# Two VectorE sums per octet ahead of a halved inverse transform, and another order of patch copies and statistics

## The chip, the core and the metric

The kernel runs on one core of one Trainium2 chip. A time is the device time of one execution in microseconds (us), the median of several. The engines are named TensorE (PE in the profile), VectorE (DVE), ScalarE (ACT), GpSimd (POOL) and SyncE (SP, which issues the transfers).

## What is computed

x is 16 images of 32 channels and 128 x 128 pixels, fp32. The first layer (group norm, a dynamic depthwise convolution, a 1x1 convolution, a residual) isn't touched by the change. The second layer is:

```python
hidden = jnp.einsum('oc,bchw->bohw', w_hidden, x)              # x after group norm; 192 hidden channels
hidden = conv_general_dilated(hidden, w_dw, padding='SAME', feature_group_count=192)   # 3x3, depthwise
q, k, v = jnp.split(hidden, 3, axis=1)                         # 64 channels each
q_fft = jnp.fft.rfft2(to_patch(q))                             # patches of 8 x 8
k_fft = jnp.fft.rfft2(to_patch(k))
out = jnp.fft.irfft2(q_fft * k_fft, s=(8, 8))
out_norm = (out - mean(out, channels)) / sqrt(var(out, channels) + 1e-05)
gated = v * (out_norm * norm_w + norm_b)
x = x + jnp.einsum('oc,bchw->bohw', w_out, gated)
```

The product of two spectra is complex. With a cosine part and a sine part for each frequency it needs four real products: cosine by cosine, sine by cosine, cosine by sine, sine by sine. The real part of the result is a difference of two of them, the other part a sum. Of the 64 coefficients of a patch, 60 belong to 30 pairs of mirrored frequencies, and 4 frequencies are real alone.

## The kernel before

**Two stages.** Stage one (to about 545 us) runs the first layer image by image and writes the normalised result to memory in halves of fp16 (high and low part). Stage two runs 32 units u = 0 to 31, each half an image: 64 rows, thus 8 rows of patches by 16 patches, 128 patches for each of 64 channels of Q, K and V. A unit has two parts. The *front* of unit u (function `front`, one for each engine) makes the hidden values of u and, woven into them, finishes unit u - 1 (the tail): norm over the channels, values, gating, projection, residual. The *spectral* part (function `spectral`) makes the spectra and the inverse transform of u. Every engine's order is written out by hand; engines meet only by semaphores.

**Front.** VectorE's `window(u, r)` copies patch row r (0 to 7) with its border out of the loaded half image `xs` into one of three buffers `win` (line 1102). TensorE's `hidden_group(u, g)` (line 572) multiplies a quarter of a patch row by the hidden weights, 32 groups for a unit, four for each window; ScalarE's `windows_out` (line 810) copies the result out. `window(u, r)` waits until the groups of window r - 2 in this counting, 4 (r - 2) groups, are done, since it fills the buffer that they read. Between groups TensorE runs `v_chunk` (line 587, values, 18 matmuls), `turn` (line 600, transposes the normed result of the tail) and `project` (line 609). For the tail VectorE runs, in eight pieces p: `pixel_stats` (line 1112, four instructions), `variance` (lines 1118 and 1120), `centre` (line 1125), `scale` (line 1132, behind GpSimd's power, line 456), `gate` (line 1137) and `residual` (line 1144). The turn of piece p waits for `scale(p)`.

**Spectral.** For each octet m of 8 channels TensorE makes Q's spectra (`q_octet`, line 647), then K's (`k_octet`, line 659), 32 records each. Channel c of four sits in partitions 32c to 32c + 31: 32 coefficients of the cosine kind in one column block of 128, 32 of the sine kind in the next. ScalarE copies Q's out of PSUM (line 852). VectorE makes two products per octet (line 1197, `quad` 0 and 1), each 512 elements per partition: the four real products of two spectra in four blocks of 128 of the buffer `prod`. `inverse(e)`, e = 0 to 3, turns two octets back: for each of the four blocks (`both`) eight matmuls of 256 columns accumulate into PSUM (line 676), 32 matmuls in all, each of which is two records in the trace. Inverse 0 stands behind octet 2, inverse 1 behind octet 4, inverses 2 and 3 behind octet 7, then the first `v_chunk` of the same unit. ScalarE copies the result to `Y` (line 865). `k_octet(m)` waits for the products of octet m - 2, since there are two PSUM banks for K.

`prod` has room for four octets, and products wait for the inverse that read the place before (`s_inverse_mm`). VectorE's first three window copies of unit u + 1 stand between the two products of octets 4, 5 and 6.

Of the kernel before, what the change touches and what calls it, by code (L numbers as in the profile page):

```python
# [28 lines left out]
TABLES = {"tables": (("identity", 128), ("inverse", 256), ("w_out", 64)),  # L29
# [5 lines left out]
def constants():  # L35

    p = np.arange(128)
# [4 lines left out]
    u, v = np.divmod(np.arange(64), 8)  # L42
# [3 lines left out]
    freq = np.concatenate([pairs, real[:2], pairs, real[2:]])  # L46
    sine = (np.arange(64) >= 32) & (np.arange(64) < 32 + len(pairs))
    angle = 2 * np.pi * ((u[freq][:, None] * u + v[freq][:, None] * v) % 8) / 8
    wave = np.where(sine[:, None], np.sin(angle), np.cos(angle)).reshape(64, 8, 8)
    spectra = np.zeros((9, 64, 10, 10), np.float64)  # L50
    for tap in range(9):
# [9 lines left out]
    cosines, sines = np.cos(angle), np.sin(angle)  # L61
    paired = np.arange(32)[:, None] < len(pairs)
    inverse = np.concatenate([np.where(paired, 2, 1) * cosines[:32], np.where(paired, 2 * sines[:32], 0), np.where(paired, 2 * sines[:32], 0),
                              np.where(paired, -2, 1) * cosines[32:]], axis=1) / 64
    out["inverse"] = np.tile(inverse, (4, 1)).astype(np.float32)
# [3 lines left out]
def build(nc, t, out):  # L69
# [13 lines left out]
    LAST = 2 * NB - 1  # L83
# [8 lines left out]
    with ctx:  # L92
# [4 lines left out]
        def semaphore(name):  # L97
            return ctx.enter_context(nc.semaphore(name))
# [86 lines left out]
        s_prod_ready = semaphore("prod_ready")  # L185
        s_inverse_mm = semaphore("inverse_mm")
# [277 lines left out]
        def _(pe):  # L464
# [173 lines left out]
            def spectral(u, tail):  # L638
# [25 lines left out]
                def inverse(e):  # L664
                    pe.wait_ge(s_prod_ready, 16 * u + 4 * e + 4)
                    if 0 < e < 3:
                        pe.wait_ge(s_y_ready, 16 * u + 4 * e)
                    if e == 0 and tail is not None:
                        pe.wait_ge(s_gated, 8 * u)
                        pe.wait_ge(s_t_copied, 8 * u)  # L670
                    if e == 3 and tail is not None:
                        pe.wait_ge(s_res_done, 4 * u)
                    for both in range(4):
                        for c in range(4):
                            for lam in range(2):
                                mm = pe.matmul(i_banks(e)[c][64 * lam:64 * lam + 64, 256 * (e % 2):256 * (e % 2) + 256],  # L676
                                               small["inverse"][32 * c:32 * c + 32, 64 * both:64 * both + 64],
                                               at(prod[32 * c:32 * c + 32, :], 2048 * (e % 2) + 128 * both + 64 * lam, [512, 4], [1, 64]),
                                               start=both == 0, stop=both == 3)
                    mm.then_inc(s_inverse_mm, 1)  # L680
# [202 lines left out]
        def _(dve):  # L883
# [262 lines left out]
            def front(u, tail):  # L1146
# [17 lines left out]
                for p in range(3):  # L1164
                    pixel_stats(tail, p)
                    variance(tail, p)
                    if p == 1:
                        centre(tail, 0)
                windows()
                scale(tail, 0)  # L1170
                centre(tail, 1)
                scale(tail, 1)
# [14 lines left out]

            def spectral(u, tail):
                for n in range(16):
                    m, quad = n // 2, n % 2  # L1190
                    if quad == 0:
                        dve.wait_ge(s_q_copied, 8 * u + m + 1)
                        dve.wait_ge(s_k_mm, 8 * u + m + 1)
                        if positive(4 * u + m // 2 - 1):
# [4 lines left out]
                                      at(q_sb[m % 2], 256 * quad, [0, 2], [128, 2], [1, 128]), ALU.mult).then_inc(s_prod_ready, 1)  # L1199
                    if n == 1 and tail is not None:  # L1200
                        gate(tail, 3, 1)
                    if n == 3 and tail is not None:
                        residual(tail, 3)
                    if u < LAST and n in (8, 10, 12):
                        window(u + 1, n // 2 - 4)
# [53 lines left out]
```

## Time and profile before

| | us |
|---|---|
| median of 3 runs | 2357.64 (2355.62 to 2362.33) |
| the profiled execution | 2366.28 |
| its span, first to last instruction | 2364.4 |
| TensorE busy (matmul records) | 2236.0 |
| VectorE busy | 1613.8 |
| ScalarE busy | 1454.2 |
| inverse transform, line 676, 8192 records | 255.6 |
| products, line 1197, 512 instructions | 337.2 |
| mean granted TensorE clock | 0.972 |

The span is one execution from its first to its last instruction; the profiled execution's own time is 1.9 us longer, and it lies 8.6 us above the median of the runs without a profile. Busy times of matmuls are modelled and overlap with pipelining, so start-to-start distances are safer for prices. The granted clock is 1.00 at TensorE's full 2.4 GHz and 0.50 at 1.2 GHz.

### The profile page before, as it was taken

What the parts mean: (1) busy time and instruction counts of PE and PEld (TensorE: products, weight loads), DVE (VectorE), ACT (ScalarE), POOL (GpSimd) and SP (SyncE); (2) the same over time, 40 slices, a digit from 0 to 9 for tenths busy, and PEclk for the clock granted to TensorE, in tenths of its full rate; (3) what the DMA queues carried; (4) which work ended last, traced back from release to release, by engine and by line L of the source; (5) the groups of instructions that cost most, each with busy time, mean ns of one, the idle gap of its engine ahead of it and who ended that gap; (6) DMA issues with size and microseconds to landing.
All of it is one profiled execution on the core that took longest, in us unless ns stands there. A gap on an engine that the chain in (4) does not pass through costs nothing.

```text
span 2364.4 us, 107028 instructions
## 1 busy us (share of the span) xinstructions
PE 2236.0 (95%) x48375; PEld 1443.6 (61%) x48375; DVE 1613.8 (68%) x4058; ACT 1454.2 (62%) x2629; POOL 486.3 (21%) x323
## 2 busy tenths in 40 slices
PE   7888888868999999999999999999999999999997
PEld 3333333346666666777676766667666666667664
DVE  5566766646777767767677667777777777777775
ACT  3456655566666666666666666666666666666662
POOL 1000000002222222222222222222222222222222
PEclk9889988978999999999999999999999999999999
DMA  7689888784333333333333333333333333333312
GB/s 140 168 212 234 226 204 219 214 200 103 75 76 76 76 76 76 79 81 76 84 73 79 76 84 80 84 81 84 76 84 76 83 78 76 76 76 76 76 43 50
DMA packets 60409, 248.63 MB, mean 105 GB/s; under 512 B 12393, under 2 KB 12658, under 8 KB 53810
## 3 DMA queue, kind: packets, MB, share of 16 engines
q1 hardware_dynamic: 59954, 241.78, 43.3%
q8 instruction: 381, 6.24, 1.1%
q14 instruction: 74, 0.61, 0.1%
HBM read 140.02 MB, written 101.72 MB: 102 GB/s over the span
## 4 chain that ended last, share of the span: by engine, by line
PE 84%; DVE 7%; ACT 4%; issue 4%; DMA 1%; SPq 0%; POOL 0%; POOLq 0%; ACTq 0%
PE bank L587 18%; PE bank L527 16%; PE bank L676 11%; PE bank L659 10%; PE bank L647 9%; PE bank L572 7%; PE bank L600 7%; PE bank L609 5%; DVE arena L1112 3%; ACT arena L865 2%; DVE arena L1132 1%; DVE arena L1125 1%; ACT arena L819 1%; DVE arena L1102 1%; ACT arena L724 1%
## 5 line engine op out<-in xcount | busy, mean ns | idle before, releaser
L456 POOL TENSOR_TENSOR arena<-arena 128x8 f32<-128x8 f32 x256 | 462.1, 1805 | 1357.6 <-DVE arena L1118 1352.6
L587 PE MATMUL bank<-arena 128*64 128x512 f16 x4608 | 689.9, 393 | 0.0
L810 ACT ACTIVATE arena<-bank 100x512 f32<-100x512 f32 x1024 | 606.6, 628 | 95.4 <-PE bank L572 75.1
L1197 DVE TENSOR_TENSOR arena<-bank,arena 128x512 f32<-128x512 f32 x512 | 337.2, 687 | 207.8 <-issue 174.0
L572 PEld LDWEIGHTS bank<-arena 128*36 128x36 f16 (+1 forms) x8192 | 330.5, 104 | 232.4 <-issue 23.5
L527 PE MATMUL bank<-arena 32*32 32x508 f32 (+1 forms) x9216 | 382.9, 649 | 55.4 <-issue 40.6
L572 PE MATMUL bank<-arena 128*36 128x128 f16 (+1 forms) x8192 | 390.5, 221 | 17.4 <-DVE arena L1102 11.5
L819 ACT ACTIVATE arena<-bank,arena 128x256 f32<-128x256 f32 x512 | 261.1, 560 | 119.9 <-PE bank L600 119.4
L852 ACT ACTIVATE arena<-bank 128x512 f32<-128x512 f32 x256 | 153.2, 598 | 265.7 <-PE bank L647 265.2
L1112 DVE BATCH_NORM_STATS2 arena<-arena 128x6 f32<-128x128 f32 x1024 | 221.7, 279 | 121.3 <-ACT arena L865 121.3
L647 PE MATMUL bank<-arena 100*32 100x128 f32 x8192 | 277.5, 274 | 5.2 <-issue 3.9
L659 PE MATMUL bank<-arena 100*32 100x128 f32 x8192 | 278.3, 274 | 0.7 <-issue 0.7
L1137 DVE TENSOR_TENSOR arena<-arena,bank 128x512 f32<-128x512 f32 x256 | 175.3, 685 | 145.9 <-ACT arena L819 145.8
L865 ACT ACTIVATE arena<-bank 128x256 f32<-128x256 f32 x512 | 155.3, 391 | 185.6 <-PE bank L676 185.6
L587 PEld LDWEIGHTS bank<-arena 128*64 128x64 f16 x4608 | 206.3, 109 | 96.0 <-ACT arena L865 10.5
L527 PEld LDWEIGHTS bank<-arena 32*32 32x32 f32 x9216 | 142.4, 107 | 194.9 <-issue 163.6
L659 PEld LDWEIGHTS bank<-arena 100*32 100x32 f32 x8192 | 222.0, 109 | 55.5 <-issue 26.4
L676 PE MATMUL bank<-arena 32*64 32x256 f32 x8192 | 255.6, 380 | 0.2
L647 PEld LDWEIGHTS bank<-arena 100*32 100x32 f32 x8192 | 220.4, 109 | 21.2 <-issue 5.0
L676 PEld LDWEIGHTS bank<-arena 32*64 32x64 f32 x8192 | 180.8, 129 | 50.3 <-issue 16.8
L600 PEld LDWEIGHTS bank<-arena 128*128 128x128 f32 x1024 | 133.7, 195 | 119.3 <-DVE arena L1132 88.7
L600 PE MATMUL bank<-arena 128*128 128x128 f32 x1024 | 181.4, 300 | 18.1 <-DVE arena L1132 10.9
(112 smaller groups left out, 1605.1 us busy)
## 6 DMA issues: line engine op xcount, KB each, us to landing
arena<-xn_d SPq DMA_DIRECT2D x128, 536.2 KB, 4.8
xn_d<-arena SPq DMA_DIRECT2D x130, 260.0 KB, 4.5
x_d<-arena SPq DMA_DIRECT2D x64, 512.0 KB, 8.3
arena<-x_d SPq DMA_DIRECT2D x128, 256.0 KB, 4.2
out<-arena SPq DMA_DIRECT2D x128, 256.0 KB, 2.7
arena<-x_in SPq DMA_DIRECT2D x32, 544.0 KB, 9.6
arena<-x_in SPq DMA_DIRECT2D x32, 528.0 KB, 9.4
arena<-spectra_in SPq DMA_DIRECT2D x1, 384.0 KB
```

The costliest lines, as they stand in the source:

```text
L456: pool.tensor_tensor(tiny["rstd"][:, slot], tiny["var_eps"][:, slot], powers, ALU.pow).then_inc(s_root, 1)
L527: mm = pe.matmul(at(psum_of(t, r)[32 * c:32 * c + 32, :], low, [W, 4], [1, high - low]), conv_w[b % 2][32 * r:32 * r + 32, 32 * tap:32 * t ...
L572: mm = pe.matmul(ring[g % len(ring)][low:high, 128 * i:128 * i + 128], w[:, first + low:first + high], hidden_w, start=True, stop=True)
L587: mm = pe.matmul(v_banks[chunk % 3][64 * s:64 * s + 64, :], v_w[:, 64 * tap:64 * tap + 64], at(xs[u % 3], row * WP + 32 * k + dx, [32 * WP ...
L600: tr = pe.transpose(t_bank[:, 128 * i:128 * i + 128], at(Y, 8 * k + 4 * jr + i, [32, 128]), ident)
L647: mm = pe.matmul(q_bank[32 * c:32 * c + 32, first:first + 128], G_q[0:WIN, 64 * ch + 32 * part:64 * ch + 32 * part + 32], hwin[0:WIN, 128 ...
L659: mm = pe.matmul(k_banks[m % 2][32 * c:32 * c + 32, first:first + 128], G_k[0:WIN, 64 * ch + 32 * part:64 * ch + 32 * part + 32], hwin[0:W ...
L676: mm = pe.matmul(i_banks(e)[c][64 * lam:64 * lam + 64, 256 * (e % 2):256 * (e % 2) + 256], small["inverse"][32 * c:32 * c + 32, 64 * both: ...
L810: act.activation(h_rows[0:WIN, :, first:first + 4], ring[g % len(ring)][0:WIN, :].rearrange("p (i c) -> p c i", i=4), ACT.Copy).then_inc(s ...
L819: ins = act.activation(at(gated[jr], 256 * lam, [32, 8], [8, 4], [1, 8]), at(banks[4], 64 * lam, [8, 8], [128, 4], [1, 8]), ACT.Identity, ...
L1112: ins = dve.bn_stats(T["pixel_stats"][:, first:first + 6], at(Y, 2048 * s + 4 * p + j, [32, 64], [1, 2]))
L1197: dve.tensor_tensor(prod[:, first:first + 512].rearrange("p (a b x) -> p a b x", a=2, b=2), at(k_banks[m % 2], 256 * quad, [128, 2], [0, 2 ...
```

## The change

VectorE gets a new function `spectrum(u, m)` behind the two products of each octet. It waits for its own products (`s_prod_ready`), then issues two instructions of 256 elements per partition (two blocks of 128, one for each of two groups of channels): a `scalar_tensor_tensor` that multiplies the fourth block by a sign per partition (-1 for the 30 pairs, 1 for the two real frequencies in the block) and adds the first, and a `tensor_tensor` that adds the second and third. Both write in place, and the second signals the new semaphore `s_spectrum`. `inverse(e)` waits for that instead of `s_prod_ready` and runs over two blocks instead of four: 16 matmuls instead of 32. The real frequencies' table rows are recast as half sums and half differences so that the same two sums serve them; the table `inverse` has 128 columns instead of 256, and one column `cross_sign` is new.

On VectorE two orders change as well. The first three window copies of the next unit stand behind all products of the unit instead of between those of octets 4 to 6. And in the front's beginning, where three sets of statistics came first, the fourth window copy (r = 3) now stands behind the first set, and the second and third set stand behind the first centring and the second one. TensorE's, ScalarE's, GpSimd's and SyncE's order of steps is the same.

```diff
+        s_spectrum = semaphore("spectrum")
...
                 def inverse(e):
-                    pe.wait_ge(s_prod_ready, 16 * u + 4 * e + 4)
+                    pe.wait_ge(s_spectrum, 8 * u + 2 * e + 2)
...
-                    for both in range(4):
+                    for part in range(2):
                         for c in range(4):
                             for lam in range(2):
...
-                                               start=both == 0, stop=both == 3)
+                                               start=part == 0, stop=part == 1)
...
-                for p in range(3):
-                    pixel_stats(tail, p)
-                    variance(tail, p)
-                    if p == 1:
-                        centre(tail, 0)
+                pixel_stats(tail, 0)
+                variance(tail, 0)
                 windows()
+                centre(tail, 0)
+                pixel_stats(tail, 1)
+                variance(tail, 1)
                 scale(tail, 0)
                 centre(tail, 1)
+                pixel_stats(tail, 2)
+                variance(tail, 2)
                 scale(tail, 1)
                 windows()
...
+            def spectrum(u, m):
+
+                first = 1024 * (m % 4)
+                dve.wait_ge(s_prod_ready, 16 * u + 2 * m + 2)
+                dve.scalar_tensor_tensor(at(prod, first, [512, 2], [1, 128]), at(prod, first + 384, [512, 2], [1, 128]),
+                                         small["cross_sign"], at(prod, first, [512, 2], [1, 128]), ALU.mult, ALU.add)
+                dve.tensor_tensor(at(prod, first + 128, [512, 2], [1, 128]), at(prod, first + 128, [512, 2], [1, 128]),
+                                  at(prod, first + 256, [512, 2], [1, 128]), ALU.add).then_inc(s_spectrum, 1)
...
+                    if quad == 1:
+                        spectrum(u, m)
                     if n == 1 and tail is not None:
                         gate(tail, 3, 1)
                     if n == 3 and tail is not None:
                         residual(tail, 3)
-                    if u < LAST and n in (8, 10, 12):
-                        window(u + 1, n // 2 - 4)
+                if u < LAST:
+                    for r in range(3):
+                        window(u + 1, r)
```

VectorE, octets 5 and 6 of a unit's spectral part, before: the products (line 1197) with a window copy (line 1102) between each two.

```order
L1197 TENSOR_TENSOR arena<-bank,arena 128x512 [waits inverse_mm,k_mm,q_copied]
L1102 COPY arena<-arena 128x1600 [waits hidden_mm]
L1197 TENSOR_TENSOR arena<-bank,arena 128x512
L1197 TENSOR_TENSOR arena<-bank,arena 128x512 [waits inverse_mm,k_mm,q_copied]
L1102 COPY arena<-arena 128x1600 [waits hidden_mm]
L1197 TENSOR_TENSOR arena<-bank,arena 128x512
```

VectorE, the last octet and what follows it, now; line numbers of the changed kernel (1207 the products, 1193 and 1195 the sums, 1101 the window copy, 1111 the statistics).

```order
L1207 TENSOR_TENSOR arena<-bank,arena 128x512 [waits inverse_mm,k_mm,q_copied]
L1207 TENSOR_TENSOR arena<-bank,arena 128x512
L1193 SCALAR_TENSOR_TENSOR arena<-arena 128x2x128 [waits prod_ready]
L1195 TENSOR_TENSOR arena<-arena 128x2x128
L1101 COPY arena<-arena 128x1600 [waits xs_in1,hidden_mm]
L1101 COPY arena<-arena 128x1600 [waits hidden_mm] x2
L1111 BN_STATS arena<-arena 128x6 [waits y_ready]
```

The sums follow each pair of products behind a wait for them, and the three copies follow the last sums.

VectorE, the beginning of the front, before, from the end of the first set of statistics to the first scaling (line 1132).

```order
L1118 TENSOR_SCALAR arena<-arena 128x8 [waits pixel_stats]
L1120 COPY arena<-arena 128x8
L1112 BN_STATS arena<-arena 128x6 x4
L1118 TENSOR_SCALAR arena<-arena 128x8 [waits pixel_stats]
L1120 COPY arena<-arena 128x8
L1125 TENSOR_TENSOR arena<-arena 128x128x4 [waits pixel_mean]
L1112 BN_STATS arena<-arena 128x6 x4
L1118 TENSOR_SCALAR arena<-arena 128x8 [waits pixel_stats]
L1120 COPY arena<-arena 128x8
L1102 COPY arena<-arena 128x1600 [waits hidden_mm]
L1132 TENSOR_TENSOR arena<-arena 128x128x4 [waits y_centred,root]
```

The same place now (each of these lines has a number one lower).

```order
L1117 TENSOR_SCALAR arena<-arena 128x8 [waits pixel_stats]
L1119 COPY arena<-arena 128x8
L1101 COPY arena<-arena 128x1600 [waits hidden_mm]
L1124 TENSOR_TENSOR arena<-arena 128x128x4 [waits pixel_mean]
L1111 BN_STATS arena<-arena 128x6 x4
L1117 TENSOR_SCALAR arena<-arena 128x8 [waits pixel_stats]
L1119 COPY arena<-arena 128x8
L1131 TENSOR_TENSOR arena<-arena 128x128x4 [waits y_centred,root]
```

The copy, with its wait for hidden groups, moved ahead of the second statistics, and one set of statistics moved behind the first scaling.

TensorE, the end of the spectral part, before: K of the last octet, the inverses 2 and 3, the values.

```order
L659 MATMUL bank<-arena 32x128 [waits prod_ready]
L659 MATMUL bank<-arena 32x128 x15
L676 MATMUL bank<-arena 64x256 [waits y_ready,prod_ready]
L676 MATMUL bank<-arena 64x256 x31
L676 MATMUL bank<-arena 64x256 [waits res_done,prod_ready]
L676 MATMUL bank<-arena 64x256 x31
L587 MATMUL bank<-arena 64x512 [waits y_ready]
```

And now:

```order
L658 MATMUL bank<-arena 32x128 [waits prod_ready]
L658 MATMUL bank<-arena 32x128 x15
L675 MATMUL bank<-arena 64x256 [waits y_ready,spectrum]
L675 MATMUL bank<-arena 64x256 x15
L675 MATMUL bank<-arena 64x256 [waits res_done,spectrum]
L675 MATMUL bank<-arena 64x256 x15
L586 MATMUL bank<-arena 64x512 [waits y_ready]
```

The steps stand as before; each inverse has half its matmuls and waits for the sums.

## Rows read from the trace of the kernel before

**Rows 1.** The page's costliest groups: the inverse (busy us, mean ns, idle before).

```profile
L676 PE MATMUL bank<-arena 32*64 32x256 f32 x8192 | 255.6, 380 | 0.2
```

**Rows 2.** Spectral, front: length; busy PE, PEld, DVE, ACT, POOL; clock; DMA.

```profile
1448.00:1472.60 24.60, 24.41 (x778) 19.78 (x777) 14.26 (x23) 10.46 (x24) 0.00 (x0) 1.00 0.23 50
1472.60:1504.40 31.80, 31.47 (x448) 19.30 (x440) 26.06 (x77) 26.02 (x48) 14.48 (x8) 1.00 0.43 102
```

**Rows 3.** TensorE in order of time: start, us, line, shape, records, idle before.

```profile
1456.59 2.00 PE L676 MATMUL bank<-arena 32*64 32x256 f32 x64
1458.52 1.08 PE L659 MATMUL bank<-arena 100*32 100x128 f32 x32
1459.42 1.06 PE L647 MATMUL bank<-arena 100*32 100x128 f32 x32
...
1467.95 1.06 PE L659 MATMUL bank<-arena 100*32 100x128 f32 x32
1468.94 3.74 PE L676 MATMUL bank<-arena 32*64 32x256 f32 x128
1472.61 2.26 PE L587 MATMUL bank<-arena 128*64 128x512 f16 x18
```

**Rows 4.** VectorE in order of time, products and gate of the same spectral part.

```profile
1451.22 1.29 DVE L1197 TENSOR_TENSOR arena<-bank,arena 128x512 f32<-128x512 f32 x2 [0.64 <-issue]
1452.43 0.68 DVE L1137 TENSOR_TENSOR arena<-arena,bank 128x512 f32<-128x512 f32 x1
```

**Rows 5.** VectorE: a step behind its own predecessor; an operand from memory.

```profile
1445.54 0.69 DVE L1125 TENSOR_TENSOR arena<-arena 128x512 f32<-128x512 f32 x1
1446.33 0.70 DVE L1132 TENSOR_TENSOR arena<-arena 128x512 f32<-128x512 f32 x1
...
34.73 0.21 DVE L1022 TENSOR_SCALAR arena<-arena 128x1 f32<-128x1 f32 x1
34.86 0.68 DVE L947 BATCH_NORM_STATS2 arena<-arena 128x6 f32<-128x512 f32 x1
```

**Rows 6.** VectorE, then TensorE, at the beginning of the front.

```profile
1474.04 0.87 DVE L1112 BATCH_NORM_STATS2 arena<-arena 128x6 f32<-128x128 f32 x4 [3.62 <-ACT arena L865]
1474.95 0.17 DVE L1118 TENSOR_SCALAR arena<-arena 128x8 f32<-128x8 f32 x1
...
1477.82 0.57 DVE L1102 COPY arena<-arena 128x1600 f16<-128x1600 f16 x1
1478.31 0.69 DVE L1132 TENSOR_TENSOR arena<-arena 128x512 f32<-128x512 f32 x1
...
1481.86 0.68 DVE L1137 TENSOR_TENSOR arena<-arena,bank 128x512 f32<-128x512 f32 x1
...
1475.83 0.40 PE L572 MATMUL bank<-arena 128*64 128x128 f16 x8
1479.05 0.71 PE L600 MATMUL bank<-arena 128*128 128x128 f32 x4 [0.33 <-DVE arena L1132]
...
1483.64 0.65 PE L587 MATMUL bank<-arena 128*64 128x512 f16 x4
```

**Rows 7.** TensorE behind idle gaps, and busy us and granted clock thereafter.

```profile
73.08 1.07 PE L527 MATMUL bank<-arena 32*32 32x508 f32 x7 [1.58 <-issue]
...
73.60:77.00 3.40, 3.40 (x48) 0.94 (x35) 0.53 (x4) 0.00 (x0) 0.89 (x2) 0.50 1.00 225
...
80.40:83.80 3.40, 3.40 (x65) 0.81 (x33) 0.45 (x1) 3.40 (x6) 0.00 (x0) 0.55 0.18 40
...
560.77 0.43 PE L647 MATMUL bank<-arena 100*32 100x128 f32 x8 [2.90 <-issue]
...
561.70:565.10 3.40, 3.40 (x74) 2.34 (x74) 1.29 (x2) 0.36 (x1) 0.00 (x0) 0.56 0.02 5
565.10:568.50 3.40, 3.40 (x106) 2.16 (x92) 0.00 (x0) 2.03 (x8) 0.00 (x0) 1.00 0.02 5
...
2325.39 0.71 PE L600 MATMUL bank<-arena 128*128 128x128 f32 x4 [1.56 <-DVE arena L1132]
```

More of the change, by code:

```diff
@@ L26 @@
 TINY = 1e-30
-TABLES = {"tables": (("identity", 128), ("inverse", 256), ("w_out", 64)),
+TABLES = {"tables": (("identity", 128), ("inverse", 128), ("w_out", 64), ("cross_sign", 1)),
           "weights": (("quarter_mean", 128), ("eye", 32), ("w1", 128), ("w2", 4), ("dyn_w", 36), ("conv1", 32),
@@ L45, in constants @@
     pairs = np.flatnonzero(mirror > np.arange(64))
[L46 to L49, printed above, removed]
+    angle = 2 * np.pi * ((u[:, None] * u + v[:, None] * v) % 8) / 8
+    cosine, sine = np.cos(angle), np.sin(angle)
+    half_sum, half_diff = (cosine[real[:2]] + cosine[real[2:]]) / 2, (cosine[real[:2]] - cosine[real[2:]]) / 2
+    wave = np.concatenate([cosine[pairs], half_sum, sine[pairs], half_diff]).reshape(64, 8, 8)
     spectra = np.zeros((9, 64, 10, 10), np.float64)
@@ L60, in constants @@
     out["row_mask"] = np.pad(np.repeat(row[:, None] == np.arange(8), 64, axis=1), ((0, 24), (0, 0))).astype(np.float32)
[L61 to L65, printed above, removed]
+    inverse = np.concatenate([2 * cosine[pairs], 2 * half_sum, 2 * sine[pairs], 2 * half_diff]).reshape(2, 32, 64)
+    out["inverse"] = np.tile(np.concatenate([inverse[0], inverse[1]], axis=1) / 64, (4, 1)).astype(np.float32)
+    out["cross_sign"] = np.tile(np.where(np.arange(32) < len(pairs), -1, 1)[:, None], (4, 1)).astype(np.float32)
     return out
@@ L676, in inverse @@
                                 mm = pe.matmul(i_banks(e)[c][64 * lam:64 * lam + 64, 256 * (e % 2):256 * (e % 2) + 256],
-                                               small["inverse"][32 * c:32 * c + 32, 64 * both:64 * both + 64],
-                                               at(prod[32 * c:32 * c + 32, :], 2048 * (e % 2) + 128 * both + 64 * lam, [512, 4], [1, 64]),
-                                               start=both == 0, stop=both == 3)
+                                               small["inverse"][32 * c:32 * c + 32, 64 * part:64 * part + 64],
+                                               at(prod[32 * c:32 * c + 32, :], 2048 * (e % 2) + 128 * part + 64 * lam, [512, 4], [1, 64]),
+                                               start=part == 0, stop=part == 1)
                     mm.then_inc(s_inverse_mm, 1)
```

## The prediction, made before the changed kernel ran

> **What bounds the kernel now.** I read the page first: the inverse matmuls of line 676 are 8192 records with 255.6 us of modelled time [rows 1]. A share of the whole span says little, so next I read the busy times of one unit in the second stage. There are 32 units (16 images, two halves), some 56.4 us each. The spectral part lasts 24.6 us and the front part 31.8 us; TensorE is busy 24.41 and 31.47 of these, VectorE 14.26 and 26.06, and the granted clock is 1.00 in both [rows 2]. So TensorE sets the pace throughout, and VectorE has 10 us free in exactly the part where the change gives it work. The third view, TensorE in order of time at the end of that spectral part, gives the prices. One inverse step holds TensorE from 1456.59 to 1458.52, 1.93 us; two in a row from 1468.94 to 1472.61, 3.67 us; one group of 32 records for Q or K takes 0.90 us from start to start [rows 3].
>
> **What is removed.** Each inverse step has half the matmuls. From the two prices, a step is 3.67 / 2 = 1.83 us and a change of kind costs 0.1 us more. Half is 0.92 us, so one unit loses 4 x 0.92 = 3.67 us of TensorE, and 32 units lose 117 us. That would be the gain if TensorE never had to wait.
>
> **What is added on VectorE.** Per octet (8 channels, two products) there are now two more instructions of 256 elements per partition, the first behind a wait for VectorE's own products. A product starts every 0.60 us (two of them 1.29, one 0.69) [rows 4]. A 512-element operation lasts 0.69 us and an 8-element one 0.17 [rows 5, 6], so 256 elements last 0.43; the next starts 0.09 us before the end, as with the products, thus 0.34 us after the start. An instruction that waits for VectorE's own predecessor starts 0.10 us behind its end (1445.54 + 0.69, then 1446.33), not 0.09 before it, so the wait costs 0.19 [rows 5]. The per-partition sign is an operand from memory: an operation with one, at 34.73, lets its successor in after 0.13 us; without one I would take 0.07, since its duration is 0.21 [rows 5]. The fused multiply-add of that size isn't in the trace. Its bounds are 0.34 (no price for the operand) and 0.69 (as dear as 512 elements); I take 0.40, since line 1022 is the nearest row. An octet is then 0.60 + 0.79 + 0.40 + 0.34 = 2.13 us on VectorE, where it was 1.2. TensorE needs 1.8 us for the Q and K of an octet, so VectorE now falls behind between the inverses.
>
> **The spectral part, followed in order.** Times count from the start of Q at 1448.13 in the unit of [rows 2]. The first product starts at 3.09, as before [rows 4]. Octet 0 ends its issue at 5.22; the gate product (line 1137) now stands behind its sums and runs at 5.22 instead of 4.30 [rows 4]. The projection waits for it only with its second half, and TensorE loses nothing. Octet 1 runs at 5.81, the residual at 7.94, octets 2, 3 and 4 at 8.54, 10.67 and 12.80. The sums for inverse 0 are there at 8.02 (TensorE wants them at 8.46), those for inverse 1 at 12.88 (wanted at 13.16). On TensorE, each shorter inverse moves all that follows forward by 0.92: K of octet 5, 6 and 7 end at 15.25, 17.10 and 19.06. VectorE takes octet 5 at 15.37, 6 at 17.50 and 7 at 19.63, by then 0.45 us behind. Inverse 2 runs from 18.97 to 19.9. Inverse 3 needs the sums of octet 7: 19.63 + 0.60 + 0.79 + 0.40 + 0.42 = 21.84, and with 0.1 us of hand-over it starts at 21.93. **TensorE stands idle for 2.0 us** between the last two inverses, where it had no gap [rows 3]. Inverse 3 ends at 22.87, where both ended at 24.48: the spectral part gains 1.61 us, not 3.67. With the bounds of the multiply-add, 0.34 gives 1.8 and 0.69 gives some -0.3 (0.29 us more in each of eight octets, of which the 0.44 us that VectorE waits before octet 5 absorbs a part).
>
> **The window copies** leave the products (three of 0.57 us, some 0.5 each in the queue) and stand behind them, from 21.76 to 23.3. VectorE would otherwise wait there until about 24.3 for inverse 3 and ScalarE's copies. Cost nothing; TensorE wants the first window some 2 us later, behind the values' matmuls. If that cover were gone they would cost 1.5 us a unit.
>
> **The front part's new order** puts a window copy behind the first statistics. Before, three sets of statistics came first: they began at 1474.04, the copy at 1477.82, the first scaling at 1478.31, and TensorE's turn of it at 1479.05, after a wait of 0.33 [rows 6]. The copy reuses the buffer of the oldest window, thus waits for the fourth hidden group (index 3), which ends at 1475.83 + 0.40 = 1476.23 [rows 6]. The statistics before it are over at about 1475.10. So VectorE now waits 1.2 us in a place where it never waited: window 1476.35, centring 1476.84, second statistics 1477.44, scaling 1478.50, 0.19 later than before although one set of statistics less stands in front. I charge 0.2 us a unit, 31 times. Further on VectorE runs 1.0 us late. The step with the least room is the first gate: it ends at 1481.86 + 0.68 = 1482.54, and the values that need it start at 1483.64 [rows 6]. Its 1.1 us just cover the delay, so nothing more is charged; if they didn't, it would be up to 1 us a unit. SP's queue has the same order of transfers, with waits on the same steps. The last front part, without windows, gains 1.2 us once, since its wait of 1.56 us for the first scaling [rows 7] mostly goes.
>
> Sum so far: 32 x 1.61 - 31 x 0.2 + 1.2 = 46.5 us.
>
> **What the new gap does to the clock.** This term halves the gain. In the first stage and the end TensorE has idle gaps of every length, and I compared each with the granted clock behind it. After the gap of 1.58 us at 73.08 the next stretch has 0.50; after the 2.90 us at 560.77, matmuls of the spectral part itself run at 0.56 on average from 561.70 on, for 3.4 us, then at 1.00; after 1.56 us at 2325.39 the clock stays full [rows 7]. Of eight gaps between 1.4 and 1.9 us that began at the full clock, from 73.08 to 2325.39, five were followed by the lower level (1.2 GHz) and three were not. All nine between 2.5 and 6 us were, and none of about 1.2 us. The new gap of 2.0 us lies between these sets. I take 6 in 10, 19 to 20 of 32 units. A stretch like that of 561.70 costs half of 3.4 us, 1.7; part of it falls into the rest of the gap, so 1.6. That is 32 us: the work it slows (inverse 3, values, hidden groups) is bound by TensorE, and nothing hides it. The net gain is 46.5 - 32 = 14.5 us. Against the profiled execution's own 2366.28 us that is 2352; the median of the runs shown is 8.6 us lower, and the second stage, where all this lies, repeats unit by unit, so I subtract from the median: **2343 us**, -0.6%.
>
> The Trainium skill (TensorE: Matmul & The Clock Gate, "Why this matters for your kernels") asks only that TensorE's idle gaps between bursts of matmuls stay under some 3 us, and by that rule a gap of 2.0 us would leave the clock alone. The rows contradict it here, with gaps of 1.58 and 2.90 us before 0.50. By the rule the time would be the first rival's.
>
> **Rivals.** (1) The gap costs no clock. For it: three of the eight short gaps; the units' matmuls use more of the array's rows than the first stage's. Against it: five of eight, and a unit of the same code at 560.77. It gives 2357.6 - 46.5 = 2311; with the cheaper multiply-add 2305. (2) Slower: the low clock outlives one stretch. After 73.60 it holds for three stretches of 3.4 us with TensorE busy in all [rows 7]. If the values and hidden groups don't bring it back at once, a second stretch costs 1.7 us more, thus 19 x 3.3 = 63 us: 2357.6 - 46.5 + 63 = 2374. It decides from 1.45 us lost per unit on average. Against it: after 561.70 one stretch was enough. (3) VectorE is dearer than priced. With the multiply-add at 0.69 the spectral part is 0.3 us slower than before, and its longer gap draws the clock down too: 2357.6 + 32 x 0.3 + 5 + 32, about 2404. Only the far bound supports it. (4) The change does nothing because another engine holds the unit: with TensorE at 24.41 of 24.6 us that is hardly possible, 2358.
>
> **How the numbers follow.** Chances: forecast 0.46, rival (1) 0.28, (2) 0.18, (3) 0.04, (4) 0.04. The range reaches from 2305 (rival 1 at its cheap bound) to 2370, most of the way to rival (2), and leaves out the rest of it and rival (3). The forecast's own range is 2325 to 2358 (from 4 to 9 units in 10 hit, hand-overs 0.1 us off). A measurement of this kernel tells 0.3%, 7 us, from no change. Faster: 0.28, 0.38 of the forecast's 0.46 and 0.02 of the rest, 0.68. Same: 0.07 of the forecast, 0.03 of rival (2) and 0.03 of (4), 0.13. Slower: 0.19.
>
> **What would show it.** In the changed profile: 4096 records for the inverse; an idle time of about 2.0 us before the fourth inverse, released by VectorE's second sum; sums that last 0.43 and 0.49 us; a wait of VectorE for the hidden groups before the fourth window; granted clock under 1.00 in most 57 us slices of the second stage, and a mean near 0.96 instead of 0.97. It is wrong if the gap is under 1.4 us, or if units with the gap keep 1.00 throughout.

## The result: slower, 2391.6 us

| | before | changed |
|---|---|---|
| median, us | 2359.59 (2355.62 to 2362.33, 4 runs) | 2391.57 (2384.37 to 2398.07, 4 runs) |
| ratio | | 1.0126 (1.0102 to 1.015) |
| span of the profiled execution | 2364.4 | 2388.1 |
| mean granted clock | 0.972 | 0.960 |

The forecast was 2343 (2305 to 2370). What was forecast for the inverse, the idle gap and the clock is in the trace; some 48 us more are there too. (Of the ten executions of e10 below one ran slow, at a granted clock of 0.557 in 3389 us; the ratios leave it out.) The changed kernel's page, costliest groups; line numbers are one lower than before up to line 1160. First the inverse (as in [rows 1]), then ScalarE's copy of the hidden groups, then the statistics:

```profile
L675 PE MATMUL bank<-arena 32*64 32x256 f32 x4096 | 157.5, 414 | 56.4 <-DVE arena L1195 55.1
L809 ACT ACTIVATE arena<-bank 100x512 f32<-100x512 f32 x1024 | 691.8, 751 | 80.6 <-PE bank L571 77.7
L1111 DVE BATCH_NORM_STATS2 arena<-arena 128x6 f32<-128x128 f32 x1024 | 265.5, 323 | 47.5 <-ACT arena L864 47.5
```

The same two groups on the page of the kernel before:

```profile
L810 ACT ACTIVATE arena<-bank 100x512 f32<-100x512 f32 x1024 | 606.6, 628 | 95.4 <-PE bank L572 75.1
L1112 DVE BATCH_NORM_STATS2 arena<-arena 128x6 f32<-128x128 f32 x1024 | 221.7, 279 | 121.3 <-ACT arena L865 121.3
```

The inverse has half its records, and 55.1 us of idle time before it that VectorE's second sum ends. That was expected. But instructions that the change doesn't touch have become dearer: ScalarE's copy by 123 ns, one statistics instruction by 44 ns. Nothing in the forecast prices that.

**The spectral part** (the end on TensorE; the second gate and the projection that stands early in it; the end on VectorE; one unit at full clock; it answers to [rows 3, 4]):

```profile
1068.72 1.06 PE L658 MATMUL bank<-arena 100*32 100x128 f32 x32
1069.71 1.13 PE L675 MATMUL bank<-arena 32*64 32x256 f32 x32
1072.67 1.13 PE L675 MATMUL bank<-arena 32*64 32x256 f32 x32 [1.83 <-DVE arena L1195]
1073.73 2.27 PE L586 MATMUL bank<-arena 128*64 128x512 f16 x18
...
1055.72 0.68 DVE L1136 TENSOR_TENSOR arena<-arena,bank 128x512 f32<-128x512 f32 x1
1056.14 1.39 PE L608 MATMUL bank<-arena 128*64 128x512 f32 x4
...
1070.48 1.28 DVE L1207 TENSOR_TENSOR arena<-bank,arena 128x512 f32<-128x512 f32 x2
1071.79 0.48 DVE L1193 SCALAR_TENSOR_TENSOR arena<-arena 128x256 f32<-128x256 f32 x1
1072.20 0.42 DVE L1195 TENSOR_TENSOR arena<-arena 128x256 f32<-128x256 f32 x1
1072.53 1.54 DVE L1101 COPY arena<-arena 128x1600 f16<-128x1600 f16 x3
```

The last octet's products end at 1071.76, the sums follow at 1071.79 and 1072.20, and the last inverse starts 0.05 us behind them after 1.83 us of idle time. From the start of Q to the values (1050.56 to 1073.73) it is 23.17 us, where the kernel before took 24.48 in the unit of the rows and 24.2 to 24.9 in its neighbours. The window copies run in VectorE's free time.

The projection of the tail (line 608) takes longer too. Before, in the same place, 5.57 us behind the start of Q:

```profile
1453.70 1.08 PE L609 MATMUL bank<-arena 128*64 128x512 f32 x4
```

The gate product now stands behind the sums of octet 0 and ends at 1056.40, so the projection's second half starts at 1056.45, 0.32 us behind the first, where before the two started within 0.01 us. The K octet behind the projection starts 6.90 us after Q instead of 6.58. So 0.32 us of the 1.6 forecast are lost here, in every unit.

**The front part** of the next unit, VectorE, then TensorE (it answers to [rows 6]):

```profile
1075.16 1.05 DVE L1111 BATCH_NORM_STATS2 arena<-arena 128x6 f32<-128x128 f32 x4 [1.08 <-ACT arena L864]
...
1077.51 0.58 DVE L1101 COPY arena<-arena 128x1600 f16<-128x1600 f16 x1 [1.02 <-PE bank L571]
...
1084.69 0.68 DVE L1136 TENSOR_TENSOR arena<-arena,bank 128x512 f32<-128x512 f32 x1
...
1080.63 0.71 PE L599 MATMUL bank<-arena 128*128 128x128 f32 x4 [0.68 <-DVE arena L1131]
...
1085.42 0.65 PE L586 MATMUL bank<-arena 128*64 128x512 f16 x4
...
1088.62 1.67 PE L608 MATMUL bank<-arena 128*64 128x512 f32 x4
```

The window copy waits for its hidden group, as forecast. Four statistics last 1.05 us instead of 0.87. TensorE waits 0.68 us at the first turn (0.33 before); the first gate ends at 1085.37, 0.05 before the values that need it, which had 1.1 us of room; the first projection spans 1.67 us, 1.03 in the kernel before, because it waits for the second gate. The front lasts 33.25 us instead of 31.95. So **a unit at full clock takes 56.42 us, what it took before (56.38)**: 1.3 us won in the spectral part, 1.3 lost in the front.

**The clock.** Two stretches of the changed kernel around its gap, [rows 7] for comparison: one unit with the low clock, one without.

```profile
1469.70:1473.10 3.40, 1.57 (x48) 0.97 (x56) 3.36 (x8) 1.22 (x4) 0.00 (x0) 0.95 0.36 83
1473.10:1476.50 3.40, 3.40 (x39) 1.40 (x26) 1.64 (x6) 1.22 (x4) 0.00 (x0) 0.55 0.34 80
1476.50:1479.90 3.40, 3.40 (x64) 2.00 (x60) 1.45 (x6) 2.20 (x4) 1.64 (x1) 1.00 1.10 254
...
1069.70:1073.10 3.40, 1.57 (x52) 0.98 (x56) 3.33 (x9) 1.22 (x4) 0.00 (x0) 1.00 0.26 57
1073.10:1076.50 3.40, 3.40 (x74) 1.94 (x57) 2.27 (x9) 1.46 (x5) 0.00 (x0) 1.00 0.68 160
```

The gap is the same in both. Behind the one the granted clock is at its lower level (1.2 GHz) for 3.4 us and the unit takes 58.02 us, behind the other it stays at 2.4. All of units 1 to 31 have the gap, and 20 of them have such a stretch; 20 x 1.6 = 32 us, all of the loss. (Unit 0 has no tail and another pattern of gaps; stretches are counted in units 1 to 31 from here on.)

### The profile page after: what moved, and what is told of

Read it like the earlier page. It is cut to its first block, busy times and chain, and to the rows that moved or that the text cites. A ratio compares the mean times of both kernels' runs of the same rounds, so it can differ in the third digit from the quotient of the medians.

```text
span 2388.1 us, 99348 instructions
## 1 busy us (share of the span) xinstructions
PE 2191.1 (92%) x44279; PEld 1360.5 (57%) x44279; DVE 1868.8 (78%) x4570; ACT 1531.1 (64%) x2629; POOL 495.1 (21%) x323
## 4 chain that ended last, share of the span: by engine, by line
PE 73%; DVE 18%; issue 5%; ACT 3%; DMA 1%; POOL 0%; SPq 0%; ACTq 0%; DVEq 0%; POOLq 0%
PE bank L586 19%; PE bank L526 16%; PE bank L658 7%; PE bank L571 7%; PE bank L608 6%; PE bank L646 6%; PE bank L599 5%; DVE arena L1207 5%; PE bank L675 5%; DVE arena L1111 4%; DVE arena L1131 2%; DVE arena L1124 2%; DVE arena L1195 2%; DVE arena L1101 1%; DVE arena L1136 1%
## 5 line engine op out<-in xcount | busy, mean ns | idle before, releaser
L455 POOL TENSOR_TENSOR arena<-arena 128x8 f32<-128x8 f32 x256 | 470.9, 1839 | 1374.2 <-DVE arena L1117 1373.8
L809 ACT ACTIVATE arena<-bank 100x512 f32<-100x512 f32 x1024 | 691.8, 751 | 80.6 <-PE bank L571 77.7
L586 PE MATMUL bank<-arena 128*64 128x512 f16 x4608 | 708.9, 403 | 4.8 <-DVE arena L1136 1.0
L1207 DVE TENSOR_TENSOR arena<-bank,arena 128x512 f32<-128x512 f32 x512 | 328.7, 684 | 54.0 <-issue 53.0
L1111 DVE BATCH_NORM_STATS2 arena<-arena 128x6 f32<-128x128 f32 x1024 | 265.5, 323 | 47.5 <-ACT arena L864 47.5
L586 PEld LDWEIGHTS bank<-arena 128*64 128x64 f16 x4608 | 212.5, 112 | 121.2 <-issue 40.7
L675 PE MATMUL bank<-arena 32*64 32x256 f32 x4096 | 157.5, 414 | 56.4 <-DVE arena L1195 55.1
L1131 DVE TENSOR_TENSOR arena<-arena 128x512 f32<-128x512 f32 x256 | 189.8, 742 | 21.0 <-POOL arena L455 1.2
```

What stands on the lines that cost most here:

```text
L455: pool.tensor_tensor(tiny["rstd"][:, slot], tiny["var_eps"][:, slot], powers, ALU.pow).then_inc(s_root, 1)
L586: mm = pe.matmul(v_banks[chunk % 3][64 * s:64 * s + 64, :], v_w[:, 64 * tap:64 * tap + 64], at(xs[u % 3], row * WP + 32 * k + dx, [32 * WP ...
L809: act.activation(h_rows[0:WIN, :, first:first + 4], ring[g % len(ring)][0:WIN, :].rearrange("p (i c) -> p c i", i=4), ACT.Copy).then_inc(s ...
L1111: ins = dve.bn_stats(T["pixel_stats"][:, first:first + 6], at(Y, 2048 * s + 4 * p + j, [32, 64], [1, 2]))
L1207: dve.tensor_tensor(prod[:, first:first + 512].rearrange("p (a b x) -> p a b x", a=2, b=2), at(k_banks[m % 2], 256 * quad, [128, 2], [0, 2 ...
```

## The experiments

The theories: **address** (the small tables shrank by 127 columns, so all buffers behind them in the arena moved by 127 fp32 words, an odd number, and accesses there cost more), against **contention** (VectorE's new work slows ScalarE and the front); **clock** (the gap itself brings the low level), against another cause; and what each of the two changed orders costs. The column `pad` is never read. Each kernel was timed beside the kernel before on the same chip; the ratios compare across the groups. Low stretches are counted in one profiled execution of each kernel. In these executions unit 1 starts its Q at anything from 584 to 600 us, e1 at 584 and the changed kernel at 594, so some 10 us between two single traces can come from stage one; unit lengths are the surer measure.

### e1 to e4: addresses and clock

e1, on the changed kernel:

```diff
-TABLES = {"tables": (("identity", 128), ("inverse", 128), ("w_out", 64), ("cross_sign", 1)),
+TABLES = {"tables": (("identity", 128), ("inverse", 128), ("w_out", 64), ("cross_sign", 1), ("pad", 127)),
```

> The changed kernel with 127 unused columns behind its small tables, so that everything behind them in the arena lies at the address it had in the kernel before (the change alone moved it by 127 fp32 words, an odd number). Address theory: ScalarE's copy of the hidden groups goes from 751 ns back to 628, the statistics from 323 to 279, a unit at full clock from 56.4 us to about 55.1, and the time from 2391.6 to about 2353; some 20 units still meet the low clock. Rival (VectorE's new load slows ScalarE and the front by contention): durations and time stay, about 2391.

Measured: 2336.19 us, ratio 0.9909 (0.9892 to 0.9927). The page has the old durations again:

```profile
L810 ACT ACTIVATE arena<-bank 100x512 f32<-100x512 f32 x1024 | 608.3, 632 | 103.0 <-PE bank L572 84.7
L1112 DVE BATCH_NORM_STATS2 arena<-arena 128x6 f32<-128x128 f32 x1024 | 221.8, 278 | 40.1 <-ACT arena L865 40.1
```

The same work at other addresses is 55 us faster than the changed kernel by the medians, 51 by the ratios. Front 32.29, spectral 23.15, unit 55.44 us. Contention falls. That this came out below the 2353 expected is in the main the clock: 10 low stretches, not some 20. From the Q of unit 1 to the Q of unit 31 the two traces differ by 45.9 us: 30 x 0.98 for the units and 1.6 for each of the ten stretches fewer. The other 5 to 9 us of the medians' difference aren't traced to a cause.

e2, on the kernel before:

```diff
-TABLES = {"tables": (("identity", 128), ("inverse", 256), ("w_out", 64)),
+TABLES = {"tables": (("identity", 128), ("inverse", 256), ("w_out", 64), ("pad", 1)),
```

> The kernel before with one unused column behind its small tables: everything behind them moves by 4 bytes, nothing else changes. Address theory: ScalarE's copy goes from 628 to about 751 ns, the statistics from 279 to 323, and the time from 2358 to some 2370 to 2395. Rival (contention from the new sums): nothing changes, 2358.

Measured: 2376.39 us, ratio 1.0092 (1.0066 to 1.0119), with no low stretch in these units.

```profile
L811 ACT ACTIVATE arena<-bank 100x512 f32<-100x512 f32 x1024 | 685.5, 751 | 62.1 <-PE bank L573 59.9
L1113 DVE BATCH_NORM_STATS2 arena<-arena 128x6 f32<-128x128 f32 x1024 | 265.0, 323 | 119.5 <-ACT arena L866 119.5
```

One unused column costs the old kernel 20 us, and the two durations are to the nanosecond those of the changed kernel. The front is 32.53 instead of 31.95.

e3 is e1 with `("pad", 1)`.

> The changed kernel with one unused column: the front's buffers then start at a multiple of 16 bytes, where the kernel before has them 8 bytes past one and the changed kernel 12 bytes past one. If groups of 8 bytes matter, durations are as in e1 (628 and 279 ns), time about 2353. If lines of 16 bytes matter, ScalarE's copy, which writes four fp32 side by side, is faster still than 628 ns, and the time is a few us below e1.

Measured: 2341.54 us, ratio 0.994 (0.9919 to 0.9961). Neither expectation quite: the copy is faster as 16-byte lines would have it, the time is not.

```profile
L810 ACT ACTIVATE arena<-bank 100x512 f32<-100x512 f32 x1024 | 582.2, 600 | 124.3 <-PE bank L572 93.4
L1112 DVE BATCH_NORM_STATS2 arena<-arena 128x6 f32<-128x128 f32 x1024 | 221.4, 278 | 39.6 <-ACT arena L865 39.6
```

Counted from the arena's start, the front's buffers begin 0, 8 or 12 bytes past a multiple of 16 in e3, e1 and the changed kernel (the latter also in e2). ScalarE's copy writes groups of four fp32: 600, 632, 751 ns. The statistics read pairs of fp32: 278, 278, 323 ns. The 323 is a mean of two kinds. Shortest, median and longest duration of all 1024 statistics, changed kernel and kernel before:

```profile
L1111 DVE BATCH_NORM_STATS2 arena<-arena x1024: 262/330/404, 562.3 to 2364.4; 128x6 f32<-128x128 f32 x171
L1112 DVE BATCH_NORM_STATS2 arena<-arena x1024: 267/277/296, 568.9 to 2340.6; 128x6 f32<-128x128 f32 x171
```

Of the four instructions of a piece the first and third read pairs that begin 12 bytes past a multiple of 16 and reach over the next one; they last 368 ns on average. The second and fourth read pairs that begin at 4; they last 277. Before, at 8 and 0, they last 281 and 277. So in one and the same kernel only the reads that cross a multiple of 16 bytes are dear.

A unit takes 55.41 us, as in e1, with 12 low stretches against 10.

e4, on e1:

```diff
-                    for part in range(2):
+                    for part in (0, 1, 0, 1) if e == 2 else (0, 1):
```

> As e1, and the third inverse of each unit (the one ahead of the idle gap) is done twice over, same values: 0.92 us more of matmuls in a gap of 1.8 us. It does more work than e1 and none earlier. Clock theory (the gap draws the clock down in about 20 units, 1.6 us each): no low stretches in the second stage, 32 us faster than e1, about 2321. Rival (low stretches have another cause, or cost nothing): as e1 or slower, 2353.

Measured: 2327.9 us, ratio 0.9869 (0.9849 to 0.9889): 8 us faster than e1, beside it on the same chip, with 32 x 0.92 us more of matmuls. The gap, and the second stage's busy times and clock:

```profile
1498.43 2.00 PE L676 MATMUL bank<-arena 32*64 32x256 f32 x64
1501.39 1.13 PE L676 MATMUL bank<-arena 32*64 32x256 f32 x32 [0.96 <-DVE arena L1196]
...
600.00:1200.00 600.00, 582.76 (x12104) 399.91 (x12094) 502.91 (x1264) 397.95 (x784) 161.56 (x88) 1.00 0.35 82
1200.00:1800.00 600.00, 582.54 (x12188) 401.17 (x12186) 501.79 (x1257) 394.29 (x779) 158.03 (x86) 1.00 0.35 81
```

No low stretch in these units, every unit some 55.44 us. The clock theory holds: with the gap cut to 0.96 us the stretches are gone, with 1.83 some units have one. The size was expected for 20 stretches; e1 has 10. From the Q of unit 1 to that of unit 31 e4 is 13.5 us shorter than e1; the medians differ by 8, and e4's stage one was 7.6 us longer in the profiled execution.

### e5 to e7: the two orders

e5 is e1 with the first hunk of the change in `front` undone: three statistics, then the window copy.

> As e1_shifted_back, with the front's beginning in the order of the kernel before (three sets of statistics, then the fourth window copy). My theory: the new order costs a wait of VectorE for the fourth hidden group, 32.29 us a front where the order before has 31.94; so the front returns to about 31.95 and the time is 11 us below e1 (2336), about 2325, give or take 10 for how many units meet the low clock. Rival (the front's 0.35 us come from VectorE's load, not from this order): front and time stay at 32.3 and 2336.

Measured: 2322.0 us, ratio 0.9843 (0.9827 to 0.9859). Front 31.95, unit 55.10; 7 low stretches. The new order costs 0.34 us a unit. At the shifted addresses it costs more: e2 has the old order and a front of 32.53, the changed kernel the new one and 33.25, a difference of 0.72.

e6 is e1 with the window copies back between the products:

```diff
-                if u < LAST:
-                    for r in range(3):
-                        window(u + 1, r)
+                    if u < LAST and n in (8, 10, 12):
+                        window(u + 1, n // 2 - 4)
```

> As e1_shifted_back, with the three window copies back between the products of octets 4 to 6. My theory: VectorE is the bound at the end of the spectral part, so 3 x 0.49 us stand in the chain ahead of the last inverse: spectral part 23.15 + 1.0 to 1.5 us, idle gap 2.8 to 3.3 us, the low clock in nearly all units, 30 x 1.2 + 20 x 1.6, thus 2385 to 2410. Rival (VectorE has enough room there): 2336.

Measured: 2403.26 us, ratio 1.0182 (1.0145 to 1.0219).

```profile
1478.75 1.13 PE L676 MATMUL bank<-arena 32*64 32x256 f32 x32
1482.46 1.85 PE L676 MATMUL bank<-arena 32*64 32x256 f32 x32 [2.58 <-DVE arena L1196]
...
600.00:1200.00 600.00, 562.52 (x11342) 380.29 (x11332) 477.94 (x1194) 375.08 (x746) 149.22 (x81) 0.97 0.34 78
1200.00:1800.00 600.00, 565.56 (x11152) 380.23 (x11150) 482.18 (x1221) 382.54 (x751) 158.44 (x87) 0.97 0.34 77
```

The gap is 2.58 us in the unit shown, 2.80 in most and 2.36 to 3.14 in all from unit 1 to 30. Each of these 30 units has a low stretch and takes 58.0 us. (The last unit has no window to copy; its gap is 1.83 and its clock stays full.) Moving the copies behind the products is worth 67 us beside e1 by the medians, 64 by the ratios.

e7 is e1 with this beginning of the front:

```diff
                 pixel_stats(tail, 0)
                 variance(tail, 0)
-                windows()
                 centre(tail, 0)
                 pixel_stats(tail, 1)
                 variance(tail, 1)
+                windows()
                 scale(tail, 0)
```

> As e1_shifted_back, with the fourth window copy behind the second set of statistics, where its hidden group is done. My theory: the first scaling comes some 0.6 us earlier than in either order and TensorE's wait at the first turn goes, front 32.29 to about 31.65, time 20 us below e1, about 2316 give or take 10 for the low clock. Rival: another wait takes its place and the front stays above 31.9.

Measured: 2311.11 us, ratio 0.9794 (0.9774 to 0.9815). Front 31.61, 3 low stretches. VectorE's first scaling and TensorE's first turn:

```profile
1446.60 0.69 DVE L1132 TENSOR_TENSOR arena<-arena 128x512 f32<-128x512 f32 x1
...
1447.78 0.71 PE L600 MATMUL bank<-arena 128*128 128x128 f32 x4
```

The scaling ends at 1447.29, half a microsecond before TensorE gets to the turn, and the wait is gone.

### e8 and e12: the last inverse without sums

e8 is e7 with, besides a table of four blocks `[cos, sin, sin, sign * cos]`:

```diff
-                    pe.wait_ge(s_spectrum, 8 * u + 2 * e + 2)
+                    if e < 3:
+                        pe.wait_ge(s_spectrum, 6 * u + 2 * e + 2)
+                    else:
+                        pe.wait_ge(s_prod_ready, 16 * u + 16)
...
-                    for part in range(2):
+                    for part in range(2 if e < 3 else 4):
...
-                    if quad == 1:
+                    if quad == 1 and m < 6:
```

> e7 and, for the last inverse of each unit, no sums: it runs over four blocks as in the kernel before, with a table that matches. TensorE does 0.92 us more, VectorE four sums fewer at the end. My theory: the gap ahead of the last inverse falls from 1.8 us to 0.5 to 0.9, no unit meets the low clock, the spectral part is 22.6 us (23.15 in e1), and the time is 2285 to 2300. Rival (the gap is not the reason of the low clock, or the extra matmuls eat the gain): e7's time or above.

Measured: 2286.22 us, ratio 0.9694 (0.9674 to 0.9714), the lowest median of all.

```profile
1202.54 1.12 PE L680 MATMUL bank<-arena 32*64 32x256 f32 x32
1204.07 2.00 PE L680 MATMUL bank<-arena 32*64 32x256 f32 x64 [0.41 <-DVE arena L1212]
1206.00 0.88 PE L588 MATMUL bank<-arena 128*64 128x512 f16 x6
```

The gap is 0.41 us, the spectral part 22.60, no low stretch. Halving three inverses of four beats halving all.

e12 is e8 with one unused column instead of three.

> e8_last_four with the front's buffers at a multiple of 16 bytes (one unused column instead of three). ScalarE's copy falls from 632 to 598 ns. The front is bound by TensorE there, so no change of the time: 2286 give or take 5. If ScalarE holds back some hidden groups, 2 to 10 us less.

Measured: 2289.3 us, ratio 0.9681 (0.9636 to 0.9727). The copy takes 600 ns (633 in e8), and the time is the same, as the first case has it.

### e9 to e11: which buffer, and whether the terms add

e9 is e1 with one word taken ahead of `hwin` and one ahead of `Y`:

```diff
+        take(1)
         hwin = take(128 * 128)
...
+        take(1)
         Y = take(64 * 64)
```

> As e1_shifted_back, but hwin, q_sb and prod (hidden values, Q's copy, products) start 4 bytes further on; Y and all behind it stay. Address theory, by buffer: ScalarE's copy into hwin is back at 751 ns, statistics (278) and scalings (692) stay fast. If ScalarE's copy is what lengthens the front of the changed kernel (33.27 us against 32.29), the front is above 33 us and the time 25 to 35 us above e1 (2336). If VectorE's chain of statistics does it, front and time stay at 32.3 and 2336 and e10 shows them.

(With both words Y begins at a multiple of 16 bytes, as in e3, not where e1 has it; by e3 its durations are the same there.) Measured: 2346.16 us, ratio 0.9935 (0.9911 to 0.9959). Front 32.41 at full clock, so 0.12 above e1, and 13 low stretches. The time is 10 us above e1 by the medians, 6 by the ratios: neither the 25 to 35 of the one case nor the nothing of the other, but much nearer to the second.

```profile
L812 ACT ACTIVATE arena<-bank 100x512 f32<-100x512 f32 x1024 | 683.5, 751 | 75.5 <-PE bank L574 73.5
L1114 DVE BATCH_NORM_STATS2 arena<-arena 128x6 f32<-128x128 f32 x1024 | 222.0, 278 | 43.5 <-ACT arena L867 43.5
```

e10 is e1 with one word ahead of `Y` and one behind it, so that Y alone begins 12 bytes past a multiple of 16.

> As e1_shifted_back, but Y, gated, res and the late half image start 4 bytes further on; hwin and the buffers beside it stay. By buffer: ScalarE's copy stays at 632 ns, statistics go to some 323 and scalings to 740. If VectorE's chain to the first turn is what lengthens the front, it is up by 0.6 us or more and the time 20 us or more above e1; if ScalarE's copy is, the front stays at 32.3 us and the time at 2336, give or take 10.

(The text on record says that gated, res and the late half image move as well. The second word moves them by another 4 bytes.) Measured: 2362.46 us, ratio 1.0005 (0.998 to 1.003). Front 33.13.

```profile
L812 ACT ACTIVATE arena<-bank 100x512 f32<-100x512 f32 x1024 | 611.8, 634 | 105.9 <-PE bank L574 87.2
L1114 DVE BATCH_NORM_STATS2 arena<-arena 128x6 f32<-128x128 f32 x1024 | 265.0, 321 | 40.1 <-ACT arena L867 40.1
```

The first turn now waits 0.68 us (0.45 in e1) and the first projection spans 1.66 (1.24), as in the changed kernel. ScalarE's copy has the larger difference per instruction and, with Q's copy and the products moved beside it, 0.12 us of effect; VectorE's statistics, centring and scaling on Y have 0.84 of the 0.97 us. Ahead of its copies ScalarE still waits for TensorE (73.5 us in all in e9), whereas TensorE waits for what VectorE makes of Y.

e11 is the changed kernel with e4's edit.

> The changed kernel at its own addresses, with the third inverse of each unit done twice as in e4. If the address term and the clock term simply add, no unit meets the low clock, a unit takes 56.42 us, and the time is about 2391.6 - 19 x 1.6 = 2361. If the longer front has to do with the low clock, the time is below that.

Measured: 2359.54 us, ratio 0.9974 (0.9951 to 0.9997). Fronts 33.27, units 56.44 us, no low stretch. The length of a unit and the price of a stretch add as expected. The number of stretches doesn't carry over: the same filler takes away 20 here (32 us by the medians) and 10 in e1 (8 us).

## Why the prediction was wrong

| full clock, us | front | spectral | unit | low stretches |
|---|---|---|---|---|
| before | 31.95 | 24.45 | 56.38 | 0 |
| changed | 33.25 | 23.17 | 56.42 | 20 |
| e1, its addresses restored | 32.29 | 23.15 | 55.44 | 10 |
| e5, e1 with the old front | 31.95 | 23.15 | 55.10 | 7 |
| e7, the copy one set later | 31.61 | 23.15 | 54.76 | 3 |
| e8, last inverse on four blocks | 31.61 | 22.60 | 54.21 | 0 |

(Fronts run from the first values' matmul to Q's first, spectral parts from there to the next values; medians of the units without a low stretch; stretches of units 1 to 31.)

- **The step that failed is a term that the sum of 46.5 us puts at nothing.** The sum has terms for instructions added, removed and reordered, and takes all other instructions at their durations before, without a reason. The smaller tables move the buffers behind them by an odd number of words, and VectorE's steps on `Y` and ScalarE's copies got dearer. With the new order in the front that costs 0.97 us a unit, 30 us in all.
- **The front's cover was used up.** The forecast charged 0.2 us for the new order and held that the first gate's 1.1 us "just cover the delay". With e1 it is 0.34 a unit: 0.13 at the first turn (0.45 us of waiting for 0.32 in e5) and 0.21 at the first projection, which spans 1.24 us instead of 1.03. With slower statistics ahead of the gate the cover was gone, as the text had priced ("it would be up to 1 us a unit"). The two don't simply add: the order alone costs 0.34 (e1 against e5), the addresses alone 0.58 (e2 against the kernel before), both together 1.30, so 0.38 of it belongs to neither alone.
- **The spectral part** was forecast to gain 1.61 us and gained 1.3. The forecast said of the projection that waits for the second gate that "TensorE loses nothing"; it loses 0.32 us, in the changed kernel as in all the variants that keep the sums there. The halved inverse, too, was mis-sized: 1.06 us from start to start for 0.92, since the change of kind of 0.1 is paid on each. Both together bring the K of octet 5 0.4 us later than forecast. VectorE then wins some back (an octet takes 2.06 us for 2.13), and the last inverse starts at 22.11 for 21.93. The rest of the order was right: gap 1.83 us for 2.0, sums 0.49 and 0.42 us as forecast.
- **That e1 lies near the forecast is in part luck.** With the addresses restored the kernel takes 2336 us, within 0.3% of 2343. But its units gain some 14 us less than forecast (spectral part 10, front 4), and it has 10 low stretches where 19 to 20 were priced, 16 us less lost; the two errors cancel.
- **The clock term** was right in kind and in price: 1.6 us a stretch (58.02 against 56.42). That 20 units were hit for the 19 to 20 forecast is chance, since the same gap hits 10 in e1 and 3 in e7. In the changed kernel eleven stretches in a row stand 58.0 us apart; in e1, whose units are 55.44 us long, they come singly or in pairs. So the gap alone doesn't set the share. The unit's length may have to do with it (units of 56.42 us: 20 hits; 56.29 in e10: 11; 55.44: 10; 55.10: 7; 54.76: 3), but no run isolates it and each number is of one execution; what sets the share stays open, and a share read off eight gaps of the first stage couldn't tell it. (The forecast's "none of about 1.2 us" passes over the gap of 1.20 at 2348.13 in the trace before, behind which, after a further 0.55 us of idle time, the clock was at 0.50 from 2349.9.) The Trainium skill (TensorE: Matmul & The Clock Gate, "Why this matters for your kernels") permits gaps up to some 3 us; these runs contradict it: 1.83 us was enough in some units, 0.96 in none.
- **The rivals.** Rival (1), no clock loss, is out by e4 and e11. Rival (2), a second low stretch, didn't occur: all in the second stage lasted 3.4 us. The time ended beyond it for a reason that none of them had.

In sum: 32 x 1.3 us gained in the spectral part, some 11 lost by the front's order, 30 by the addresses (18 of them alone, 12 only with the new order), 32 by the clock. That makes 31 us slower; 32 were measured.

## What to carry to other kernels

List what an edit moves in memory as well as in the queues: a table that grows or shrinks ahead of others shifts them all, and one word can cost as much as an edit brings (20 us in e2, against the 21 that e1 gains on the kernel before). Where work moves from the bound engine to another, follow the last item of each loop, since there nothing is left to hide the new steps; leaving the old form for that one item can be the best split. A step that "waits only with its second half" has a price too, if its halves ran side by side before. And an idle gap of about two microseconds on TensorE can be priced twice, by itself and by the clock behind it; filling it even with useless matmuls paid here (8 us in e4, 32 in e11).

## What the runs showed of the hardware

- Access cost by start address, in bytes past a multiple of 16 from the arena's start: ScalarE writing groups of four fp32, 512 per partition out of PSUM, 600 ns at 0, 632 at 8, 751 at 12. VectorE's statistics on pairs of fp32, 278 ns at 0 and 8, 323 at 12; its scalings of groups of four in place, 690 at 0, 692 at 8, 742 at 12. The Trainium skill (SBUF — State Buffer, the note on cachelines in "Door 1: The DMA port swizzle") tells of lines of 16 bytes and a penalty for each access that goes on to another line. It also wants at least two accesses in a line for full bandwidth. Both fit: at 12 bytes each group of four is split into one and three, and ScalarE's copy and the scaling are slow; at 8 it is split into two and two, which costs ScalarE 32 ns and VectorE's scaling nothing clear; and of the statistics only those whose pairs are split are slow, 368 ns for 277.
- How much longer an instruction gets doesn't set the price here: 119 ns more on 32 ScalarE copies a unit cost 0.12 us (e9), some 40 to 50 ns more on each of VectorE's steps on `Y` 0.84 (e10).
- TensorE's granted clock fell to 0.50 for 3.4 us at gaps of 1.83 us in 3 to 20 of 31 units (e7, the changed kernel), at gaps of 2.36 to 3.14 us in all 30 of e6, at 0.41 and 0.96 us in none (e8, e4, e11). A longer gap alone doesn't decide it: ahead of the last inverse of unit 0 a gap of 2.28 to 2.38 us left the clock full in e4, e6, e8 and e11, while 2.10 in e5 was followed by the lower level.
